# A recurrent tanh kernel: the float32 tanh of half one moves to PSUM, and is subtracted and added to x1 from there

## The reference, cut to what matters

```python
def step(prev_h, xw):
    next_h = jnp.tanh(prev_h @ Wh + xw)      # xw = x1[t] @ Wx + b
    return (next_h, next_h)
_, h_t = jax.lax.scan(step, h0, xW_t)        # h0 = cond, 256 steps
return x1 + swapaxes(h_t, 0, 1)              # x1 = x * (1 + 1 + gate)
```

## Time and profile before

| | |
|---|---|
| median of 3 runs | 253.32 us (252.93 to 253.58) |
| the profiled execution | 253.53 us, span of its records 251.7 us |
| PE busy | 242.7 us (96%) |
| PE weight loads | 228.3 us (91%) |
| DVE busy | 150.8 us (60%) |
| ACT busy | 121.2 us (48%) |
| TensorE's granted clock | full from about 18 to 250 us, half from about 8 to 18 us |

### The profile page before, as it was taken

One profiled execution on the slowest core, in us unless ns is written; L12 is line 12 of the kernel. 1 busy time (PEld: TensorE's weight loads), 2 busy tenths in 40 slices (PEclk: granted clock), 3 DMA queues, 4 the chain that ended last, 5 costly groups with the idle time before them and its releaser, 6 DMA issues.

```text
span 251.7 us, 10329 instructions
## 1 busy us (share of the span) xinstructions
PE 242.7 (96%) x4220; PEld 228.3 (91%) x4220; DVE 150.8 (60%) x780; ACT 121.2 (48%) x1026; POOL 4.0 (2%) x9
## 2 busy tenths in 40 slices
PE   6499999999999999999999999999999999999995
PEld 5488999999999999999999999999999999999874
DVE  3146666666666666666666666666666666655553
ACT  2024445555555555555555555555555555555553
POOL 0310000000000000000000000000000000000000
PEclk9659999999999999999999999999999999999998
DMA  6999520020202010020202002020201002020211
GB/s 179 388 388 384 185 86 3 6 83 1 87 3 86 4 62 27 4 86 1 86 3 86 5 6 82 3 86 1 87 3 62 28 3 86 4 86 1 86 44 44
DMA packets 10877, 18.59 MB, mean 74 GB/s; under 512 B 1037, under 2 KB 2894, under 8 KB 10830
## 3 DMA queue, kind: packets, MB, share of 16 engines
q1 hardware_dynamic: 9870, 17.37, 19.0%
q10 hardware_dynamic: 960, 0.56, 0.7%
HBM read 9.54 MB, written 8.39 MB: 71 GB/s over the span
## 4 chain that ended last, share of the span: by engine, by line
PE 94%; DMA 3%; ACTq 1%; issue 0%; DVE 0%; ACT 0%; DVEq 0%
PE bank L200 59%; PE bank L195 30%; DMA wh_sb<-in_wh 3%; PE bank L188 3%; PE bank L177 1%; PE bank L183 1%; ACTq L147 0%; ACTq L146 0%; ACTq L148 0%; DVE g_t L342 0%; DVE x L298 0%; ACT tanh_z L156 0%; DVE h_t L311 0%; ACT h L166 0%; ACT h_t L167 0%
## 5 line engine op out<-in xcount | busy, mean ns | idle before, releaser
L354 DVE TENSOR_TENSOR h<-h_t,h 128x32 f16<-128x32 f32 x510 | 94.9, 192 | 88.3 <-ACT h_t L167 87.6
L200 PE MATMUL bank<-h,wh_a 128*128 128x32 f16 x1530 | 145.0, 179 | 0.8 <-ACT h L166 0.2
L200 PEld LDWEIGHTS bank<-h,wh_a 128*128 128x128 f16 x1530 | 122.4, 110 | 13.0 <-ACT h L166 7.2
L195 PE MATMUL bank<-x,wx_sb 128*128 128x128 f32 x512 | 109.8, 308 | 0.3 <-DVE x L298 0.3
L200 PE MATMUL bank<-h,wh_b 128*128 128x32 f16 x765 | 109.1, 176 | 0.0
L200 PE MATMUL bank<-h,wh_c 128*128 128x32 f16 x765 | 109.0, 176 | 0.0
L166 ACT ACTIVATE h<-bank 128x32 f16<-128x32 f32 x255 | 50.4, 198 | 115.5 <-PE bank L200 113.5
L200 PE MATMUL bank<-h_t,wh_sb 128*128 128x32 f32 x510 | 103.6, 285 | 0.0
L195 PEld LDWEIGHTS bank<-x,wx_sb 128*128 128x128 f32 x512 | 75.6, 193 | 0.8 <-issue 0.7
L200 PEld LDWEIGHTS bank<-h_t,wh_sb 128*128 128x128 f32 x510 | 75.8, 188 | 0.0
L200 PEld LDWEIGHTS bank<-h,wh_b 128*128 128x128 bf16 x765 | 68.9, 96 | 0.4
(11 more groups left out here) (31 smaller groups left out, 19.6 us busy)
## 6 DMA issues: line engine op xcount, KB each, us to landing
x<-in_x SPq DMA_DIRECT2D x16, 512.0 KB, 11.4
out_dram<-h_t SPq DMA_DIRECT2D x15, 512.0 KB, 2.7
w_t<-in_w SPq DMA_DIRECT2D x1, 256.0 KB, 2.9
w_t<-in_w ACTq DMA_DIRECT2D x1, 256.0 KB, 6.4
wx_sb<-in_wx SPq DMA_DIRECT2D x1, 256.0 KB, 7.2
wh_sb<-in_wh ACTq DMA_DIRECT2D x1, 256.0 KB, 7.3
out_dram<-h_t SPq DMA_DIRECT2D x1, 256.0 KB, 2.1
out_dram<-h_t SPq DMA_DIRECT2D x2, 128.0 KB, 2.4
```

What stands on the lines that cost most here:

```text
L195: return nc.tensor.matmul(pre[c % 2][e][m][:, steps, :], wx_sb[:, k, m * P:(m + 1) * P], moving, start=False, stop=False, skip_group_check ...
L200: return nc.tensor.matmul(pre[t // CS % 2][s % 2][m][:, s // 2, :], weights[:, k, m * P:(m + 1) * P], h_part, start=start, stop=stop, skip ...
L354: nc.vector.tensor_tensor(h2[:, t % 2, m, :], h_t[:, m, t * B:(t + 1) * B], h1[:, t % 2, m, :], ALU.subtract).then_inc(h2_ready[m], 1)
```

## The change

The float32 tanh of half 0 is no longer written to `h_t` in SBUF but to `h_first`, 32 otherwise unused columns in the PSUM bank of the same parity, slot and half as its z. The DVE subtraction of half 0 reads it there. `add_out` is split: `add_first` adds x1 to `h_first` in every step and writes `h_t`, `add_second` does half 1 for two steps at once. A new semaphore `first_added` counts the `add_first`s. PE waits for it before it writes to a bank again: in each step from 2 on ahead of the wait for `h1_ready[0]`, and in `fill` in the first chunk and at each chunk's first step. SP waits for it before each store.

```diff
--- before.py
+++ after.py
@@ -76,6 +76,8 @@
                  for e in range(2)] for s in range(2)]
         pre = [[[b[:, 0:N // 2].rearrange("p (s b) -> p s b", b=B) for b in parity] for parity in slot]
                for slot in bank]
+
+        h_first = [[slot[e][0][:, N // 2:N // 2 + B] for e in range(2)] for slot in bank]
         z_ps = [bank[1][0][m][:, N // 2:] for m in range(HALVES)]
         warm_ps = bank[0][0][0][:, N // 2:]
 
@@ -106,6 +108,7 @@
         h1_ready = [sem(f"h1_ready_{m}") for m in range(HALVES)]
         h_ready = [sem(f"h_ready_{m}") for m in range(HALVES)]
         h2_ready = [sem(f"h2_ready_{m}") for m in range(HALVES)]
+        first_added = sem("first_added")
         out_ready = sem("out_ready")
         out_stored = sem("out_stored")
 
@@ -124,6 +127,7 @@
                 if c == 0:
                     sp.dma_start(wx_sb[:], wx.rearrange("(k p) n -> p k n", p=P)).then_inc(wx_loaded, DMA)
             for first, steps in STORES:
+                sp.wait_ge(first_added, first + steps)
                 sp.wait_ge(out_ready, (first + steps) // 2)
                 cols = slice(first * B, (first + steps) * B)
                 sp.dma_start(out_view[:, :, cols], h_t[:, :, cols]).then_inc(out_stored, DMA)
@@ -164,7 +168,7 @@
                 act.wait_ge(pre_ready[0], t + 1)
                 if t < T - 1:
                     nc.scalar.activation(h1[:, t % 2, 0, :], z_t[0], ACT.Tanh).then_inc(h1_ready[0], 1)
-                nc.scalar.activation(h_t[:, 0, cols], z_t[0], ACT.Tanh).then_inc(h_ready[0], 1)
+                nc.scalar.activation(h_first[slot][s % 2], z_t[0], ACT.Tanh).then_inc(h_ready[0], 1)
                 act.wait_ge(pre_ready[1], t + 1)
                 nc.scalar.activation(h_t[:, 1, cols], z_t[1], ACT.Tanh).then_inc(h_ready[1], 1)
                 if t < T - 1:
@@ -248,6 +252,9 @@
 
             def fill(t):
                 c, s = t // CS, t % CS
+                if t > 0 and (c == 0 or s == 0):
+
+                    pe.wait_ge(first_added, t)
                 if c == 0:
                     fill_first(t)
                 elif c < CHUNKS - 1:
@@ -271,6 +278,9 @@
                     h1_last, h2_last = h1[:, (t - 1) % 2, :, :], h2[:, (t - 1) % 2, :, :]
 
 
+                    if t > 1:
+
+                        pe.wait_ge(first_added, t - 1)
                     pe.wait_ge(h1_ready[0], t)
                     if t == 1:
                         pe.wait_ge(wh_split, 1)
@@ -306,9 +316,14 @@
                 nc.vector.tensor_tensor(cols, cols, g_t[:, k, :].unsqueeze(1).to_broadcast([P, CS // 4, B]), ALU.mult)\
                     .then_inc(x1_ready, 1)
 
-            def add_out(t):
+            def add_first(t):
+                cols = slice(t * B, (t + 1) * B)
+                nc.vector.tensor_tensor(h_t[:, 0, cols], h_first[t // CS % 2][t % 2], x1[:, 0, cols], ALU.add)\
+                    .then_inc(first_added, 1)
+
+            def add_second(t):
                 cols = slice(t * B, (t + 2) * B)
-                nc.vector.tensor_tensor(h_t[:, :, cols], h_t[:, :, cols], x1[:, :, cols], ALU.add)\
+                nc.vector.tensor_tensor(h_t[:, 1, cols], h_t[:, 1, cols], x1[:, 1, cols], ALU.add)\
                     .then_inc(out_ready, 1)
 
             nc.vector.memset(ones[:], 1.0).then_inc(ones_ready, 1)
@@ -349,10 +364,15 @@
 
             for t in range(T):
                 c, s = t // CS, t % CS
-                for m in range(HALVES if t < T - 1 else 0):
-                    dve.wait_ge(h1_ready[1] if m else h_ready[0], t + 1)
-                    nc.vector.tensor_tensor(h2[:, t % 2, m, :], h_t[:, m, t * B:(t + 1) * B], h1[:, t % 2, m, :],
-                                            ALU.subtract).then_inc(h2_ready[m], 1)
+                dve.wait_ge(h_ready[0], t + 1)
+                if t < T - 1:
+                    nc.vector.tensor_tensor(h2[:, t % 2, 0, :], h_first[t // CS % 2][t % 2], h1[:, t % 2, 0, :],
+                                            ALU.subtract).then_inc(h2_ready[0], 1)
+                if t < T - 1:
+                    dve.wait_ge(h1_ready[1], t + 1)
+                    nc.vector.tensor_tensor(h2[:, t % 2, 1, :], h_t[:, 1, t * B:(t + 1) * B], h1[:, t % 2, 1, :],
+                                            ALU.subtract).then_inc(h2_ready[1], 1)
+                add_first(t)
                 if c == 0:
                     if s < PIECES:
                         scale(1, s)
@@ -361,10 +381,9 @@
                 elif s % 2 == 1 and c + 2 < CHUNKS:
                     scale(c + 2, s // 2)
                 if t % 2 == 0 and t >= 2:
-                    add_out(t - 2)
-            for m in range(HALVES):
-                dve.wait_ge(h_ready[m], T)
-            add_out(T - 2)
+                    add_second(t - 2)
+            dve.wait_ge(h_ready[1], T)
+            add_second(T - 2)
 
 
 def kernel(**inputs):
```

## The result

The changed kernel takes 263.93 us (median of 4 runs, 262.93 to 264.46) against 253.37 (4 runs, 252.93 to 253.58): a ratio of 1.0415, with a 95% interval of 1.0393 to 1.0436. It is slower, as forecast, but by 10.6 us and not by 7.0; 263.9 lies above the range. The profiled execution took 263.84, 10.3 more than the one before.

A forecast was written before the change was run, and what follows sets the result against it. The prediction took steady steps to be bound by latency, not PE's work. 228 short steps at 0.030 us gave 6.84, plus 0.15 made 7.0 us: forecast 260.4 us, range 257.3 to 262.7.

The forecast's parts named there:

- way A: Path round a steady step through half 1's float32 tanh to its float32 load; ends last, sums to the 0.89 us step.
- way B: Path through half 0's first load and six matmuls to half 1's float32 load; room 0.03 us, change adds 0.06.
- PE-bound steps: Steps in front of which fill lays two products, 1.06 us each; claimed not to pay for the separate wait.
- ACT's write to PSUM: Tanh of half 0 to PSUM: 0; half 1's float32 tanh might end 0.005 to 0.02 us earlier, loss counts beyond 0.03.
- rival 1: Separate wait hidden and ACT's queue shorter: 0.012 to 0.022 us a step gained, 248.7 to 251.0 us; chance 0.06.
- DVE's read of PSUM: Half 0's subtraction, now reading PSUM: up to 0.055 us longer, fits in room of 0.08, so 0.
- DVE's additional instruction: add_first in every step: 0 in general, as DVE has idle time; once +0.15 us at step 8 of chunk 0.

The follow-up runs named there:

- e1_wait_ahead: Kernel before, plus one long-met PE wait (h2_ready[0]) written ahead of the wait for h1_ready[0], nothing to PSUM: 263.01 us, ratio 1.038.
- e4_wait_behind: Kernel before, plus one long-met PE wait (h2_ready[0]) written behind the wait for h1_ready[0]: 253.17 us, ratio 0.9993.
- e2_waits_swapped: Changed kernel with PE's two waits in the other order, h1_ready[0] first and first_added second: 258.83 us, ratio 1.0209.
- e5_psum_first: Changed kernel with PE's waits swapped and ACT's two half 0 writes reordered, float32 to PSUM before float16 to SBUF: 266.27 us, one run.
- e3_split_only: Kernel before with only the addition split, all from SBUF, no new PE wait: 253.19 us, ratio 0.999.
- e8_two_waits: Kernel before, plus two long-met PE waits (h2_ready[0], h2_ready[1]) ahead of the wait for h1_ready[0]: 263.63 us, ratio 1.0381.
- e10_wait_on_half_one: Kernel before, plus one long-met PE wait (h2_ready[0]) ahead of the wait for h_ready[1]: 268.43 us against 254.32, ratio 1.0553.

## Why the prediction came out wrong

**The mechanism was right.** A steady step is bound by latency and not by PE's work; way A ended last with 0.03 of room for way B; the new semaphore pushed the wait on `h1_ready[0]` out of the weight load, and way B took over (e1_wait_ahead and e4_wait_behind). The PE-bound steps stayed at 1.06.

**The term that failed** is "Way B gets 0.06 longer and has 0.03 of room, so it now ends last and the step grows by 0.030". Measured, the step grows by 0.043: 9.8 us and not 6.84. The 0.06 up to the load was right (0.113 against 0.050, medians over the steady steps' records). I stopped counting there. With the wait in the load, the first matmul follows at 0.004; with the wait ahead of it, at 0.031, and 0.012 of that is still there at the sixth matmul. So way B got 0.063 + 0.012 = 0.075 longer, which less its room of 0.032 is the 0.043. Why the matmul comes later behind a separate wait is not shown by any run. The trace of before had a sign of it, though at half the clock and with a float32 load: behind the load at 14.34 the matmul starts only at 14.38, where the load at 120.63 has its own at 120.64.

```profile
14.38 0.55 PE L195 MATMUL bank<-x,wx_sb 128*128 128x128 f32 x1 [0.27 <-DVE x L298]
```

I read the load and not its matmul. The bounds were made from the load alone, so they did not take it in, and with 228 repetitions 0.012 is nearly 3 us.

**ACT's write to PSUM**: taken as 0, with a loss counting beyond 0.03. It was a loss of 0.025 (228 against 203 ns), inside the room: 0 in this kernel, but a loss of 5.3 us is left when the wait is put right (e2_waits_swapped). That the 0 held was luck as much as reasoning: against the 0.030 of the forecast, 0.005 was left. The prediction's section on this write has way A end 0.005 to 0.02 earlier if the queue gets shorter, and its rival 1 gains 0.012 to 0.022 a step from the same cause; the two don't agree, and neither came about. The gain of rival 1, which rested on the queue of writes, does not exist here. The Trainium skill (ScalarE: Activation LUTs, Step-by-step) calls PSUM the lower-latency destination: e5_psum_first agrees for a tanh behind an idle stretch, 182 against 198 ns; third in the queue or second, it gained nothing, and what followed lost.

**DVE's read of PSUM**: bounds 0 and 0.055, measured 0 (192 ns). The 65 ns that the Trainium skill (Perfetto Trace Analysis, Optimizing Scalar/DVE Operations) would add don't show, with one of two operands in PSUM. The pointer operand, and not PSUM, probably makes the 247 of L333; no run isolates that.

**DVE's additional instruction**: +0.15 at step 8, measured +0.12. Elsewhere 0, as e3_split_only shows.

**What no term had**: 0.4 us ahead of and in the loop's first step, of which 0.25 goes with a clock that rose to full 0.9 us later. The runs don't tie it to the change: with no tanh written to PSUM, the loop's first step took 2.11 us in e1_wait_ahead, where the clock rose to full at 16.2 us, and 3.20 in e8_two_waits, where it rose at 18.8.

## What to carry to other kernels

An instruction keeps one of its semaphore waits; the others go into an instruction ahead of it. In a loop bound by latency look which one that is: if the last to be met goes through the separate one, it costs about 0.06 us up to the load and may cost more behind it. Here the order of two lines in the source decided which wait became the separate one. When a second wait on PE is needed, write the one that ends last first, and count a stage to the point where it meets the other way, not to its first instruction.

## What the hardware did that I had not expected

- A weight load that is released by a wait of its own has its matmul 0.004 us behind it (before, e4_wait_behind); behind a separate wait that was met last it is 0.031 (e1_wait_ahead, after). In e10_wait_on_half_one, with a float32 load, it is 0.031 too, against 0.002 before, but the matmuls after it came no later behind the load.
- A separate wait held two semaphores in one instruction of 51 ns; the third semaphore of a step cost nothing (e8_two_waits and e1_wait_ahead, a ratio of 1.038 each).
- A tanh of 128x32 to SBUF that is third in a row takes 228 ns directly behind one to PSUM that is itself second in a row, and 203 behind one to SBUF; the one to PSUM takes 182 when it stands first and 192 when second.
- A subtraction of 128x32 on DVE takes 192 ns with one of its two operands in PSUM, and with both in SBUF.
